# Experts that fetch their tokens by a list and add their answers into the output, in place of a sorted copy of all rows

## What is computed

```python
norm = layer_norm(feat, ln_g, ln_b)          # feat: the layer-normed x, (T, D)
scores = norm @ centroids.T
for e in range(E):                           # balanced_assignment
    s = where(taken, -inf, scores[:, e])
    _, idx = top_k(s, C); parts.append(idx); taken = taken.at[idx].set(True)
sort_by_expert = concatenate(parts)
routed = feat[sort_by_expert].reshape(E, C, D)
h = layer_norm(routed, ln_g, ln_b)
h = gelu(einsum('ecd,edf->ecf', h, w1) + b1)
h = einsum('ecf,efd->ecd', h, w2) + b2
out = routed + h                             # back in token order, added to x
```

## Time and profile before

| | |
|---|---|
| median of 3 runs | 2394.24 us (2392.93 to 2397.34) |
| the profiled execution | 2394.96 us |
| its span, first to last instruction | 2393.2 us |
| TensorE / VectorE / ScalarE busy | 69% / 61% / 58% of the span |
| GpSimd busy | 6% of the span |
| mean granted TensorE clock | 0.743 of full speed |

### The profile page before, as it was taken

How to read it: one execution, slowest core, us unless ns; L and a number is a source line. 1 busy time by engine, 2 the same in 40 slices (tenths; PEclk the granted TensorE clock), 3 DMA queues, 4 the chain that set the end, 5 groups by cost and what they waited for, 6 DMA issues and landing times. The chain is left out here.

```text
span 2393.2 us, 22586 instructions
## 1 busy us (share of the span) xinstructions
PE 1649.6 (69%) x6426; PEld 712.0 (30%) x6426; DVE 1468.5 (61%) x3457; ACT 1398.1 (58%) x2634; POOL 143.8 (6%) x127
## 2 busy tenths in 40 slices
PE   4788599999997344778877787777867774122091
PEld 2443244444443001222323222332222222122061
DVE  5554353535344799787797878877787507487211
ACT  4464243434332596989989899798989763000030
POOL 0000000000001000000000000000000000144505
PEclk9898799999998555665567666676666796555596
DMA  3000255555553101101010110201001000200322
GB/s 133 1 0 0 51 151 141 142 144 141 146 149 79 56 24 47 64 19 60 21 72 33 35 54 15 91 20 43 36 31 48 21 28 4 37 0 1 114 62 79
DMA packets 55773, 143.12 MB, mean 60 GB/s; under 512 B 7888, under 2 KB 22608, under 8 KB 53040
## 3 DMA queue, kind: packets, MB, share of 16 engines
q1 hardware_dynamic: 52448, 136.56, 18.9%
q0 software_dynamic: 2048, 4.20, 0.6%
q10 hardware_dynamic: 1152, 0.92, 0.3%
HBM read 124.22 MB, written 17.43 MB: 59 GB/s over the span
## 5 line engine op out<-in xcount | busy, mean ns | idle before, releaser
L1435 DVE CUSTOM_DVE_ANT_0 sa_lg<-sa_e,sa_lg 128x1024 f32<-128x1024 f32 (+7 forms) x512 | 387.1, 756 | 163.7 <-ACT sa_lg L1347 163.5
L1215 PE MATMUL sa_ps<-sa_k1s,sa_q1s 72*128 72x512 bf16 (+3 forms) x768 | 295.8, 454 | 233.6 <-DVE sa_nmax L1426 197.9
L1337 ACT ACTIVATE sa_e<-sa_e,sa_nmax 128x1024 f32<-128x1024 f32 (+7 forms) x512 | 401.2, 784 | 48.5 <-DVE sa_nmax L1426 48.2
L1426 DVE CUSTOM_DVE_ANT_0 sa_e<-sa_ps,sa_mask 128x1024 f32<-128x1024 f32 (+7 forms) x512 | 385.4, 753 | 37.0 <-PE sa_ps L1215 35.3
L1347 ACT ACTIVATE sa_lg<-sa_e,sa_sum 128x1024 f32<-128x1024 f32 (+7 forms) x512 | 400.4, 782 | 2.7 <-DVE sa_prod L1435 2.2
L1355 ACT ACTIVATE sa_p<-sa_ps 128x512 f32<-128x512 f32 x576 | 337.1, 602 | 110.8 <-PE sa_ps L1249 57.5
L1246 PE MATMUL sa_ps<-sa_q2s,sa_k2s 75*128 75x512 bf16 (+3 forms) x768 | 297.4, 424 | 93.6 <-ACT sa_p L1355 71.4
L863 DVE TENSOR_TENSOR mx_hw<-mx_spread,mx_h 128x512 f32<-128x512 f32 x256 | 176.4, 691 | 251.5 <-ACT mx_h L770 242.9
L770 ACT ACTIVATE mx_h<-mx_ps 128x512 f32<-128x512 f32 (+1 forms) x264 | 156.8, 597 | 285.3 <-PE mx_ps L706 277.0
L706 PE MATMUL mx_ps<-mx_f,m 128*128 128x512 f32 x512 | 263.0, 595 | 1.3 <-ACT mx_h L770 1.3
L719 PE MATMUL mx_ps<-mx_hw,m 128*128 128x512 f32 x512 | 262.0, 594 | 1.1 <-DVE mx_hw L863 1.1
(11 more groups left out here) (306 smaller groups left out, 1894.6 us busy)
## 6 DMA issues: line engine op xcount, KB each, us to landing
mx_spread<-mx_spill SPq DMA_DIRECT2D x256, 256.0 KB, 4.0
sa_q1s<-sa_spill_q SPq DMA_DIRECT2D x96, 96.0 KB
sa_k1s<-sa_spill_k SPq DMA_DIRECT2D x96, 96.0 KB
sa_q2s<-sa_spill_q SPq DMA_DIRECT2D x48, 192.0 KB
sa_k2s<-sa_spill_k SPq DMA_DIRECT2D x48, 192.0 KB
m<-m_in SPq DMA_DIRECT2D x1, 4256.0 KB
be_w<-w_in SPq DMA_DIRECT2D x16, 256.0 KB, 6.4
sa_spill_q<-sa_qp SPq DMA_DIRECT2D x4, 768.0 KB, 12.8
```

The source lines that it names most:

```text
L1215: last = nc.tensor.matmul(out[:, col:col + w], q_ring[:, c % 2, local, i * P:(i + 1) * P], k_ring[:, c % 2, local, col:col + w], start=Tru ...
L1337: nc.scalar.activation(e[:, u % 5, 0:w], e[:, u % 5, 0:w], ACT.Exp, scale=-1.0, bias=nmax[:, b % 2, i, h:h + 1], accum_out=sums[:, b % 2, ...
L1426: nc.vector.tensor_tensor_reduce(out=e[:, u % 5, 0:w], in0=slot_of("unit", u)[:, 0:w], in1=mask_wide[:, SEQ - w:SEQ], scale=1.0, scalar=3. ...
L1435: nc.vector.tensor_tensor_reduce(out=lg[:, u % 2, 0:w], in0=e[:, u % 5, 0:w], in1=lg[:, u % 2, 0:w], scale=1.0, scalar=0.0, op0=ALU.mult, ...
```

## The change

- **Scores.** GpSimd adds `feat` to `x` per batch (4 adds of 128x1024), which VectorE did at the start of the experts. SP, after each batch's scores, stores that batch's `norm` rows to a tensor `normed` and its sum to `out` (512 KB each); the last batch's pair is issued at the end of SP's list in the assignment.
- **Assignment.** After the turned `place`, VectorE splits each slot into a low part (slot mod 128) and a high part (slot div 128), makes one-hot tiles of both, and TensorE sums 32 bf16 products that put each token's number at its slot. The result is `tokens`: for each expert the list of its tokens. `m4` grows by 129 columns.
- **Experts.** POOL gathers an expert's 512 rows of `normed` by 4 indirect transfers, three experts ahead, and adds the answers into `out` by 4 accumulating indirect transfers. The scatter to `routed`, the loads of rows, the stores and gathers of `answers`, the final adds and the stores of `out` go.

The core of the diff:

```diff
 def scores_block(...):
...
+                    if b + 1 < BATCH:
+                        sp.wait_ge(inner[b % 2].scaled.sem, b // 2 + 1)
+                        sp.wait_ge(summed.sem, b + 1)
+                        store_rows(sp, b)
...
+            @block.gpsimd
+            def _(pool):
+                for b in range(BATCH):
+                    pool.wait_ge(outer[b % 2].scaled.sem, b // 2 + 1)
+                    nc.gpsimd.tensor_tensor(x[:, seq(b), :], x[:, seq(b), :], feat[:, seq(b), :], ALU.add
+                                            ).then_inc(summed.sem, 1)
...
 def assignment_block(...):
...
+        COLS = TOKENS // P
+        CHUNKS = 4
+        WIDTH = COLS // CHUNKS
...
                 copies(sp.dma_start, keys_hi, hi, 1, SEARCHED, hi_rest)
+                store_last(sp)
...
+                for c in range(CHUNKS):
+                    pe.wait_ge(hot_ready.sem, c + 1)
+                    for k in range(c * WIDTH, (c + 1) * WIDTH):
+                        last = nc.tensor.matmul(ps[:, 0, 0:2 * COLS], one_hot[:, k, :],
+                                                listed[:, k, :, :].rearrange("p a n -> p (a n)"),
+                                                start=(k == 0), stop=(k == COLS - 1))
+                last.then_inc(list_mm.sem, 1)
...
-                nc.vector.tensor_copy(index[:, :].rearrange("p (r q) -> p r q", r=ROWS),
...
+                link(nc.vector.tensor_copy(spot[:, :].rearrange("p (r q) -> p r q", r=ROWS),
+                                           ps[:, 3, 0:COLS].rearrange("p (q r) -> p r q", r=ROWS)))
+                link(nc.vector.tensor_scalar(low_spot[:, :], spot[:, :], P - 1, None, ALU.bitwise_and))
+                link(nc.vector.tensor_scalar(high_spot[:, :], spot[:, :], 7, None, ALU.logical_shift_right))
+                link(nc.vector.tensor_copy(low_b[:, :], low_spot[:, :]))
+                link(nc.vector.tensor_copy(high_b[:, :], high_spot[:, :]))
...
+                link(nc.vector.tensor_tensor(at_high[:, :, :], across(high_b, 0, COLS, COLS), along(iota[:, 0:COLS], COLS),
+                                             ALU.is_equal))
+                link(nc.vector.tensor_tensor(listed[:, :, 0, :], at_high[:, :, :],
+                                             iota[:, 0:COLS].unsqueeze(2).broadcast_to([P, COLS, COLS]), ALU.mult))
+                link(nc.vector.tensor_scalar(listed[:, :, 1, :], at_high[:, :, :], mat(m4, MATS4, "row"), None, ALU.mult))
+                for c in range(CHUNKS):
+                    a, b = c * WIDTH, (c + 1) * WIDTH
+                    nc.vector.tensor_tensor(one_hot[:, a:b, :], across(low_b, a, b, P), along(iota, WIDTH), ALU.is_equal
+                                            ).then_inc(hot_ready.sem, 1)
+                dve.wait_ge(list_mm.sem, 1)
+                link(nc.vector.tensor_copy(inner[:, :], ps[:, 0, COLS:2 * COLS]))
+                nc.vector.scalar_tensor_tensor(out=tokens[:, :], in0=ps[:, 0, 0:COLS], scalar=float(P), in1=inner[:, :],
+                                               op0=ALU.mult, op1=ALU.add).then_inc(tokens_ready.sem, 1)
...
 def balanced_experts_block(...):
...
+    AHEAD_ROWS = 3
...
-                for t in range(COLS):
-                    pool.indirect_dma_start(routed, bass.IndirectOffsetOnAxis(ap=index[:, t:t + 1], axis=0),
-                                            norm[:, t, :], None).then_inc(scattered.sem, 16)
-                pool.wait_ge(stored.sem, 16 * E1)
-                for t in range(COLS):
-                    pool.indirect_dma_start(back[:, t, :], None, answers,
-                                            bass.IndirectOffsetOnAxis(ap=index[:, t:t + 1], axis=0)
-                                            ).then_inc(gathered[t // TILES].sem, 16)
+                def of(e, t):
+                    return bass.IndirectOffsetOnAxis(ap=tokens[:, e * SHARE_TILES + t:e * SHARE_TILES + t + 1], axis=0)
+
+                def gather(e):
+                    for t in range(SHARE_TILES):
+                        pool.indirect_dma_start(rows[:, e, t, :], None, normed, of(e, t)).then_inc(gathered[e].sem, 16)
+
+                def add(e):
+                    pool.wait_ge(ot_ready.sem, e + 1)
+                    for t in range(SHARE_TILES):
+                        pool.indirect_dma_start(out_rows, of(e, t), o_tm[:, e, t, :], None, compute_op=ALU.add
+                                                ).then_inc(added.sem, 16)
+
+                pool.wait_ge(kept, 16 * BATCH)
+                for e in range(AHEAD_ROWS):
+                    gather(e)
+                pool.wait_ge(based, 16 * BATCH)
+                for e in range(E1):
+                    if e + AHEAD_ROWS < E1:
+                        gather(e + AHEAD_ROWS)
+                    add(e)
+                pool.wait_ge(added.sem, 16 * E1 * SHARE_TILES)
...
-                sp.wait_ge(scattered.sem, 16 * COLS)
-                for e in range(E1):
-                    sp.dma_start(rows[:, e, :, :], routed_v[e]).then_inc(r_loaded[e].sem, 16)
-                for e in range(E1):
-                    sp.wait_ge(ot_ready.sem, e + 1)
-                    sp.dma_start(answers_v[e], o_tm[:, e, :, :]).then_inc(stored.sem, 16)
...
-                for b in range(BATCH):
-                    nc.vector.tensor_tensor(seq(x, b), seq(x, b), seq(feat, b), ALU.add).then_inc(sum_ready.sem, 1)
...
-                    dve.wait_ge(gathered[b].sem, 16 * TILES)
-                    nc.vector.tensor_tensor(seq(x, b), seq(x, b), seq(back, b), ALU.add).then_inc(x_ready.sem, 1)
...
+            def store_rows(sp, b):
+                seq = slice(b * TILES, (b + 1) * TILES)
+                sp.dma_start(normed_v[:, seq, :], norm[:, seq, :]).then_inc(kept, 16)
+                sp.dma_start(out[b].rearrange("(t p) c -> p t c", p=P), x[:, seq, :]).then_inc(based, 16)
```

More of the change, by code:

```diff
@@ L125 @@
     (MATS3, [("wq", CH), ("wk", CH), ("wv", CH), ("wo", CH), ("bo", CH)]),
-    (MATS4, [("cent1", 8), ("same", P), ("before", P), ("copies", 16), ("offsets", 8), ("deltas", 8)]),
+    (MATS4, [("cent1", 8), ("same", P), ("before", P), ("copies", 16), ("offsets", 8), ("deltas", 8), ("iota", P), ("row", 1)]),
 ):
@@ L1633, with scores_block @@
 TAKEN = -float(2 ** 34)
-def scores_block(nc, x, feat, norm, scores, vecs, m1, m4, eps):
+def scores_block(nc, x, feat, norm, scores, store_rows, vecs, m1, m4, eps):
     with ExitStack() as ctx:
@@ L2049, in balanced_experts_block @@
+                dve.wait_ge(tokens_ready.sem, 1)
+def balanced_experts_block(nc, tokens, normed, kept, based, w1_in, w2_in, b2_in, out, vecs, m1):
+    AHEAD_ROWS = 3
     with ExitStack() as ctx:
@@ L2278, in constants @@
               for turn in range(2) for k in range(len(STEPS))]
-    extra = {"deltas": np.stack(deltas, 1).astype(np.float32), "same": same.astype(np.float32), "before": before.astype(np.float32),
+    iota = np.arange(P, dtype=np.float32)
+    extra = {"iota": np.tile(iota, (P, 1)), "row": iota[:, None], "deltas": np.stack(deltas, 1).astype(np.float32), "same": same.astype(np.float32), "before": before.astype(np.float32),
              "copies": copies.astype(np.float32), "offsets": np.stack(offsets, 1).astype(np.float32)}
```

62 lines of the change are left out of this document (29 added, 33 removed).

## The result

The changed kernel takes 2355.38 us (median of 4 runs, 2354.1 to 2358.71) against 2393.64 for the kernel before beside it (2392.93 to 2397.34): a ratio of 0.9841, 95% interval 0.9824 to 0.9858. The forecast was 2334.2 in a range of 2326 to 2352: the time went down as forecast, but by 38 us and not by 60.

A forecast was written before the change was run, and what follows sets the result against it. POOL and TensorE were to bound the experts stage together. Experts -76.4, assignment +11.0, scores +5.0, small terms +0.4 make -60.0 us: median 2334.2 us from 2394.24, range 2326 to 2352.

The forecast's parts named there:

- Price of the accumulating add: Experts, POOL: each accumulating add costs the same as a plain scatter, 1.26 us; bounds 1.25 to 2.05.
- rival A: Experts, POOL: each accumulating add d us dearer, counted 32 times; d 0.34 gives +10 us, 0.79 gives +24.4; 27%.
- The end: End of experts: only the last add's landing follows POOL's last issue, 2.9 us, between 2.2 and 3.8.
- The overlap: Experts: POOL and TensorE work side by side, 8.05 us per expert; stage 87.4 us against 163.8, 76.4 less.
- First expert: Start of experts: rows there at 10.5 us, first answer at 23.4 us from POOL's first gather.
- The slow first transfers: Start of experts: the first two transfers stay slow, 1.4 us over the usual, though VectorE's adds go.
- The chain: Assignment, before the first gather: new VectorE and TensorE work adds 11.0 us, bounds 9.6 to 13.5.
- The lock in scores: Scores: VectorE's L86 waits 1.25 us per batch for GpSimd's add, 5.0 us in all, from 0 to 6.

The follow-up runs named there:

- two kernels in which nothing else waits: Changed kernel, 20 gathers ahead, SP's end wait, sums in assignment, one pause: 2349.71 us; and 1 KB rows, plain scatters, four experts ahead, rare pauses: 2334.72 us.
- the kernel whose transfers have the price that I had assumed: Changed kernel with its 32 accumulating adds made plain scatters, so x and feat are missing from the output: 2351.72 us, ratio 0.9815.
- Rows of 1 KB: Changed kernel with norm and x + feat stored as one row, VectorE adding them to the answer, plain scatters: 2354.27 us, 0.9828.

## Why the prediction was wrong, and where it was right

- **Price of the accumulating add: wrong, and the step that failed.** "I take the plain scatter" gave 1.26 us per add; it is 1.86. That is 19.0 us in the kernel after, and 19.2 between two kernels in which nothing else waits. It was rival A (27%) at d = 0.60, just above the 0.57 to which the range reached up. The reason against taking the plain price stood in the rival itself (an add needs the old value too). The bounds 1.25 to 2.05 held 1.86, but by luck above: the 2.05 came from a scatter that VectorE's adds had slowed, which has nothing to do with accumulating. The choice at their lower end was the error.
- **The end: wrong, 2.9 forecast, 7.5 measured.** The landing was long enough: 3.3 us, against 2.2 for a plain scatter, but counted from the start of the transfer's row, so it ends 1.75 us behind the issue. I had read landings as counted from the end of the row, throughout. What was missing is a term for the 5.7 us from the landing (2346.6) to the end of the span (2352.3), of which some 2 go when SP waits in POOL's place. What fills the rest no run shows.
- **The overlap: right in kind, on a condition that I had not named.** TensorE and POOL do work side by side, and an expert takes 8.05 us. But in the kernel whose transfers have the price that I had assumed the stage took 108.6 us, not 87.4, since the signals were held. The dear adds hid that second error: with the right price alone the forecast would have failed all the same. TensorE's clock, which I had kept at 1.00, also falls for a product behind each long wait (granted 0.50 to 0.61). Only with pauses, and with four experts gathered ahead, does the sum come out: 91.9 us, 4.5 over the forecast, 3.3 of them at the end (6.2 instead of 2.9) and 1.2 on POOL (last issue at 85.7 instead of 84.5).
- **First expert: right, with an error that cancels in part.** First answer at 21.8 to 23.5 us against 23.4. The rows were there at 9.2 us and not at 10.5 in the kernel after, since the 1.4 us of slow first transfers did not come; in its repeats TensorE's first up product took 6.0 to 6.1 us and not 5.1, and the answer 0.2 to 0.8 us more.
- **The slow first transfers: wrong, the 1.4 us went.** The first two took 1.18 and 0.97 us, not 1.57 and 1.75. The weight loads run there still, so they weren't the cause. VectorE's adds were, by the 14 transfers under "Rows of 1 KB": each waited for the two-input add that ran when it started, but for its last 0.12 us. The same count gives both slow rows: the adds of the earlier trace rows take 1.22 us each and start some 1.14 apart, so the one running at 2229.39 ends at 2229.9 (1.18 + 0.39 = 1.57), the one running at 2231.27 at 2232.2 (0.96 + 0.79 = 1.75). The gathers beside L2183 did not speak against it, since three of those four adds began while a gather ran already; the fourth began 0.03 us ahead of one, and there the add took 1.28 us and not 1.23. The Trainium skill (SBUF — State Buffer, section Who interferes with whom) has a VectorE instruction with two SBUF inputs contend with a GpSimd one that reads SBUF. The traces agree if an indirect transfer counts as one; I had counted it as none, and so kept the 1.4 us.
- **The chain: right, 9.7 against 11.0** (within 9.6 to 13.5). TensorE's tail was 0.7 instead of 1.7, L2085 0.49 instead of 0.73.
- **The lock in scores: right, 4.0 of the 5.0.** L86 waits 1.0 us each time, since GpSimd's add takes 2.35 and not 2.5. Another 2.7 us come with TensorE's clock: L1708 has a mean of 1032 ns, its like before (L1697) 935. In the stretch of the last batch the granted clock was 0.50 (1.2 GHz) in the kernel after, first fence, and 0.99 (2.4 GHz) in the kernel before, second fence:

```profile
2034.00:2041.00 7.00, 3.72 (x11) 1.81 (x11) 1.48 (x2) 2.62 (x4) 0.00 (x0) 0.50 0.56 155
```

```profile
2035.00:2041.00 6.00, 2.98 (x12) 1.14 (x12) 0.39 (x1) 2.74 (x3) 0.00 (x0) 0.99 0.05 8
```

 In the eight kernels without the sums in the scores the stage took 59.8 us (two), 61.1 to 61.3 (three) and 62.4 (three); in the nine with them 65.4 to 66.5. So time of this kind was lost beside the lock every time, and without it in six of eight. What makes the clock fall wasn't tried.

## What to carry to other kernels

Price an instruction form that the trace doesn't hold at the upper part of its bounds when it does more work than its nearest row, and above all when it stands on the queue that sets the end. Where GpSimd feeds TensorE by indirect transfers without a rest, look for "remote" waits on VectorE and ScalarE, and try half a microsecond of something else on GpSimd every ten; here that gave 12 to 16 us of the stage back, together with one more expert gathered ahead. Read which end of a row a landing is counted from. Work moved onto GpSimd is free only beside instructions of VectorE that don't contend with it: four 2.35 us adds cost 4 us in one place, 7 in another, and 3.6 when two of them fell into a wait.

## What the runs showed of the hardware

- POOL's price for an indirect transfer of 128 rows: 0.95 us for a gather of 64 or 128 KB, 0.97 for a plain scatter, 1.555 for an accumulating one (1.41 with 64 rows), each with 0.30 before the next. Landing, from the start of the row, 2.2 us for a plain scatter, 3.3 for an accumulating one. A transfer that starts inside a VectorE add with both inputs in on-chip memory waits for it: 1.05 to 1.50 us beside an add of 0.68.
- TensorE's signals: late by up to 9.3 us beside 16 to 20 plain transfers without a pause and by 23.7 beside 32; the two longest shown above were released 2.5 and 5 us behind the last transfer, one of 1.7 us came within such a row. On time in five kernels with 0.5 to 1 us of pause behind every 4 to 8 transfers, late by up to 1.7 us in a sixth with 0.97 behind every 4. Signals of DMA to VectorE came on time beside 32 plain gathers.
- In the kernel after, 32 accumulating adds and 16 gathers ran without a pause and all eight lags were 0.04 us; in its repeats single ones were 0.2 to 0.9. Why a plain transfer every 1.25 us holds the signals and one in 1.86 hardly does, whether TensorE itself is held (its instructions came with gaps too), whether the recording of the profile takes part, and whether it is the memset or POOL's wait for it that frees them, stays open.
